# Attention on one NeuronCore: where TensorE makes the values of the four batches of a tile

## The reference

```
x = normalise(x * s1)                       # over the 512 features
q = heads(x @ q_weight.T * q_dc)
k = heads(x @ k_weight.T * k_dc)
v_flat = x @ v_weight.T * v_dc * s2;  v = heads(v_flat)
attn = softmax(q @ k.T * scale)             # 128 x 128 for each batch and head
out  = (attn @ v) @ w_weight.T * w_dc
skip = v_flat @ u_weight.T * u_dc
return out + skip
```

## Time and profile before

| | |
|---|---|
| Time, three runs | 4002.31, 4001.20, 3997.74 us; median 4001.2 |
| Profiled execution: span, first to last instruction | 3993.2 us (its own device time isn't listed; the median of the runs is 8.0 above the span) |
| TensorE busy over the span | 3737.8 us, 94% |
| VectorE busy | 3026.1 us, 76% |
| ScalarE busy | 1334.5 us, 33% |
| GpSimd busy | 1896.0 us, 47% |
| Mean granted clock of TensorE | 0.959 |

### The profile page before, as it was taken

How to read it: one execution, slowest core, us unless ns; L and a number is a source line. 1 busy time by engine, 2 the same in 40 slices (tenths; PEclk the granted TensorE clock), 3 DMA queues, 4 the chain that set the end, 5 groups by cost and what they waited for, 6 DMA issues and landing times. The chain is left out here.

```text
span 3993.2 us, 63716 instructions
## 1 busy us (share of the span) xinstructions
PE 3737.8 (94%) x22068; PEld 2291.3 (57%) x22068; DVE 3026.1 (76%) x3176; ACT 1334.5 (33%) x2014; POOL 1896.0 (47%) x1446
## 2 busy tenths in 40 slices
PE   8999769999998789999999999988999859999999
PEld 6777523433333567777777777766777613433334
DVE  4776679999997677777777777744666679999997
ACT  3555411111111444344434444323555501111111
POOL 2655635555554124444444444342555735555554
PEclk9999859999999799999999999999999959999999
DMA  3666755565653323222322222223666765565563
GB/s 121 236 240 246 286 200 169 183 194 173 187 187 120 112 90 128 78 80 79 107 88 91 80 80 80 67 78 121 227 238 245 275 223 169 175 193 179 183 194 112
DMA packets 272125, 630.18 MB, mean 158 GB/s; under 512 B 33216, under 2 KB 35904, under 8 KB 271840
## 3 DMA queue, kind: packets, MB, share of 16 engines
q1 hardware_dynamic: 264816, 615.49, 46.3%
q10 hardware_dynamic: 7104, 11.93, 0.8%
HBM read 390.87 MB, written 241.70 MB: 158 GB/s over the span
## 5 line engine op out<-in xcount | busy, mean ns | idle before, releaser
L1164 DVE CUSTOM_DVE_ANT_0 l0r_g<-l0r_g,l0r_pv,l0r_cf 128x1024 f32<-128x1024 f32 x512 | 674.1, 1339 | 70.4 <-PE l0r_pv L964 46.7
L1164 DVE CUSTOM_DVE_ANT_0 l3r_g<-l3r_g,l3r_pv,l3r_cf 128x1024 f32<-128x1024 f32 x512 | 673.9, 1339 | 68.3 <-PE l3r_pv L964 43.6
L102 PE MATMUL l1h_ps_p<-l1h_xh,l1c_wh 128*128 128x512 f32 x768 | 322.6, 420 | 5.7 <-issue 3.5
L104 PE MATMUL l1h_ps_p<-l1h_xl,l1c_wh 128*128 128x512 f32 x768 | 308.2, 401 | 0.0
L103 PE MATMUL l1h_ps_p<-l1h_xh,l1c_wl 128*128 128x512 f32 x768 | 305.4, 398 | 0.0
L2152 POOL TENSOR_TENSOR l1h_st<-l1h_veps 128x1 f32<-128x1 f32 x64 | 35.4, 554 | 565.5 <-DVE l1h_veps L2010 565.5
L964 PE MATMUL l3r_pv<-l3r_x,l3r_wv 32*128 32x512 f32 x1024 | 260.4, 507 | 25.0 <-POOL l3r_wv L884 17.4
L964 PEld LDWEIGHTS l0r_pv<-l0r_x,l0r_wv 32*128 32x128 f32 x1024 | 97.2, 187 | 324.7 <-issue 205.0
L964 PEld LDWEIGHTS l3r_pv<-l3r_x,l3r_wv 32*128 32x128 f32 x1024 | 96.5, 186 | 324.7 <-issue 191.8
L964 PE MATMUL l0r_pv<-l0r_x,l0r_wv 32*128 32x512 f32 x1024 | 261.7, 510 | 22.5 <-POOL l0r_wv L884 16.4
L976 PE MATMUL l0r_py<-l0r_g,l0r_cd 128*32 128x512 f32 x2048 | 281.7, 624 | 0.0
(11 more groups left out here) (386 smaller groups left out, 9046.9 us busy)
## 6 DMA issues: line engine op xcount, KB each, us to landing
l0r_x<-xhl_s SPq DMA_DIRECT2D x128, 512.0 KB, 11.4
l3r_x<-xhl_s SPq DMA_DIRECT2D x128, 512.0 KB, 11.6
xhl_s<-l0a_xo SPq DMA_DIRECT2D x116, 512.0 KB, 4.6
xhl_s<-l3a_xo SPq DMA_DIRECT2D x116, 512.0 KB, 4.6
gate_s<-l0a_gate SPq DMA_DIRECT2D x64, 256.0 KB, 2.5
l0r_dx<-dx_s SPq DMA_DIRECT2D x32, 512.0 KB, 13.2
l0r_gate<-gate_s SPq DMA_DIRECT2D x32, 512.0 KB, 13.9
l0r_crow<-feed_s SPq DMA_DIRECT2D x64, 256.0 KB
```

The costliest lines, as they stand in the source:

```text
L102: pe.matmul(out, wh, xh, start=first, stop=False)
L104: return pe.matmul(out, wh, xl, start=False, stop=last)
L1164: dve._custom_dve(bass.dve_ops.TENSOR_ADD_SAT, out=g[:, t, j, :], in0=g[:, (t - 1) % TS, j, :], in1=pv[j % 2][:, :], s0=cf[:, q, t, 0, j:j ...
```

## The change

In TensorE's `period(p)` two calls move. values(g, 0) goes from ahead of turn(g, 1) to directly ahead of values(g, 1), and values(g, 2) from ahead of turn(g, 3) to directly ahead of values(g, 3). The new order is: scores; turn 0; mix_u; turn 1; mix_w; values 0; values 1; turn 2; project Q; turn 3; project K; values 2; values 3; turn_v; project V. Waits go with their calls and stay as they are. No other engine is changed.

```diff
                 if sooner(p, "K"):
                     project(p, Q, "Q", q_mm)
-                values(g, 0)
                 turn(g, 1)
                 if burst:
                     turn_x(p, "X3")
@@
                     project(p, K, "K", k_mm)
                 elif sooner(p, "Q"):
                     project(p, Q, "Q", q_mm)
+                values(g, 0)
                 values(g, 1)
                 turn(g, 2)
                 if not sooner(p, "Q"):
                     project(p, Q, "Q", q_mm)
                 if extra(p):
                     next_sum_rows(p)
-                values(g, 2)
                 turn(g, 3)
                 if not sooner(p, "K"):
                     project(p, K, "K", k_mm)
                 if extra(p):
                     next_add_rows(p)
+                values(g, 2)
                 values(g, 3)
                 turn_v(p)
                 project(p, V, "V", v_mm)
```

## The result

| | before | after |
|---|---|---|
| Median | 4001.76 us (4 runs) | 3978.39 us (4 runs) |
| Ratio | | 0.9944, 95% interval 0.9929 to 0.9958 |
| Profiled execution, span | 3993.2 us | 3981.8 us |
| First to last scores of the attention stage (rows below) | 1284.3 us | 1262.2 us |
| TensorE busy | 3737.8 us | 3707.3 us |

The forecast was 3975.7 in a range of 3969 to 3989. The change makes the kernel 0.56% faster, 22 us by the ratio (17 to 28).

A forecast was written before the change was run, and what follows sets the result against it. TensorE was taken to bound the attention stage, except burst heads, which go at VectorE's pace. 106 pairs at 0.27 us (-28.6), -0.7 for the last tiles and +3.8 paid gave -25.5: 3975.7 us, range 3969 to 3989.

The forecast's parts named there:

- What bounds the stage: Attention stage: TensorE busy 1338 of 1400 us, all of an ordinary period; time taken from its stream leaves the total.
- The group taken out, 0.51: Between mix_u and mix_w in an ordinary period: removing a values group saves 1.41 - 0.90 = 0.51 us.
- The group put in, 0.24: A values group directly beside another group costs 0.13 + 0.11 = 0.24 us, bounds 0.20 to 0.36.
- First pairs of the bursts: Values 0 leave time VectorE's pace hides in burst heads: 14 cost 0.24 us each, the weight swap's nothing.
- Periods 1, 2, 4 and 5: Second pairs: 0.24 us cost each in periods 1 and 2, nothing in 3 to 5; other pairs gain 0.27.
- Second pairs of the last tiles: Last two tiles: turn 3 goes first, values 2 run during ScalarE's last copy, saving 0.36 us each.
- The sum: Whole kernel: -28.6 - 0.7 + 3.8 = -25.5 us; by the bounds -10.8 to -30.4.
- the covers of batch 1's copy: Values 1 and turn 2 wait for ScalarE's copy of batch 1, with 1.3 us of cover.
- The time around the span: Whole execution: 8.0 us taken to lie between the profiled span of 3993.2 us and the median of 4001.2.
- Rival 1: Second values group costs 0.36 us, its weight loads not overlapping the first's matmuls; -10.8 us, 3990.4; chance 0.06.
- Rival 2: VectorE or ScalarE sets ordinary periods' pace; only the last tiles' 0.7 us stay, 4000.5; chance 0.05.
- Rival 3: Clock falls in bursts behind longer TensorE gaps: +22 us and 4023, or a loss of 24; chance 0.04.

The follow-up runs named there:

- the kernel with the groups apart: Against the kernel before: values 0 behind mix_w, then turn 2, values 1; turn 3, values 2, project K, values 3; ratio 1.0026 (1.0014 to 1.0039).
- the second timing: The changed kernel itself timed once more, nothing altered, against the kernel before; ratio 0.993 (0.9912 to 0.9948).
- one run of four groups: Against the changed kernel: ScalarE's copies kept in e, all four values groups together behind project K; ratio to the kernel before 0.992 (0.99 to 0.9941).
- the two kernels with the run next to the scores: All four values groups behind project V, copies in e: ratio 0.9907 to the kernel before; the second also copies batch 2 sooner, ratio 0.9863.
- the last kernel: Against the kernel with all values behind project V: ScalarE copies batch 2 ahead of high parts of v and o; 3951.0 us, 0.9863 to before.

## Why the prediction was right, point by point

- **What bounds the stage.** Right: TensorE is busy all of an ordinary period before and after, and what its stream lost came out of the time. "No wait is removed" was wrong by the traces, which have 64 wait instructions less (1164 for 1228); it made no difference, since the kernel with the groups apart has 96 less and is slower.
- **The group taken out, 0.51.** Right: 0.50 in the timeline.
- **The group put in, 0.24 within 0.20 to 0.36.** Measured 0.22: with values 0 alone moved the burst gets longer by it, and keeping values 0 in the burst's head takes it back. The second group's first wave has nothing of an entry in it, so my 0.13 for it was 0.02 too much. A pair brings 0.29, where I said 0.27. With the groups apart the gain is gone (19.58), so it is the change of form that is paid. The 0.29 is what the prediction worked out by the rule of the Trainium skill in TensorEngine Tiling (Array Packing), Key Properties, that TensorE is drained when the tiling mode changes and not when only the tile does; the trace agrees.
- **First pairs of the bursts.** Right in kind and size: 21.55 to 21.47 for the burst shown, +0.22 for the first pair and -0.28 for the second.
- **Periods 1, 2, 4 and 5.** The second pairs of 1 and 2 cost 0.2 each, as said. The first pairs of all four were counted at 0.27 and brought nothing: with values 0 alone moved, these periods stay within 0.1 us of before. That is 1.1 us too much in the sum.
- **Second pairs of the last tiles.** Right: period 63 of after has the order that I drew, turn 3 at 2623.93 behind the copy and values 2 right behind the turn, at 2624.49. From the last scores to the last values it is 22.96 us where it was 24.12.
- **The sum.** -25.5 forecast, -22 measured (17 to 28 less), -28 in the second timing (21 to 35 less). By the pair's measured 0.29 and 0.22 for a group that is paid it would be -28, so the number came out close in part because errors cancel. By the starts of the scores the profiled execution loses, against that sum, some 5 us at the stall of periods 47 and 48, the 1.1 of the four first pairs above, and 0.9 in period 38, which has a new wait: turn 3 stands 0.71 us for ScalarE's copy of batch 2.

```profile
2129.10 0.63 PE L1637 MATMUL l1h_ps_t<-l1h_ident,l1h_e 128*128 128x128 f32 x4 [0.71 <-ACT l1h_pt L1764]
```

VectorE does the swap's low part of W just before (3.26 us from 2115.54) and is late with that tile's softmax. I had named the covers of batch 1's copy, and not that of batch 2's for turn 3; it is what one run of four groups ran into in ordinary periods. On the other side two bursts got shorter by more than a pair's worth. Period 7 went from 25.47 us in both traces of before to 23.96 and 23.98, and period 31, with the first weights of the swap, from 27.73 to 26.54 and 25.71. In both the clock fell less: over period 7 it is 0.93 before and 1.00 after, over period 31 0.88 and 0.94 or 1.00. So it isn't one execution's luck. But I had left out that the change could raise the clock, and no run shows what in it does.
- **The time around the span.** The 8.0 us was wrong in kind: the profiled execution of after spans 3981.8 us and took 3983.86, so 2 us lie around it. By the same 2 us (an estimate) before's profiled execution took about 3995, less than any of its timed runs. This did not touch the forecast, since span and 8.0 add up to the median.
- **Rival 1** (the second group's weight loads don't overlap with the first group's matmuls, 0.36): out. Two groups need 0.22 more than one and not 0.36, and all 16 loads of a run lie within 0.38 us, beside matmuls that span 0.64:

```profile
1924.14 0.38 PEld L1647 LDWEIGHTS l1h_ps_o<-l1h_pt,l1h_v 128*32 128x32 f32 x16 [0.36 <-issue]
```

The sentence in the Trainium skill, TensorE: Matmul & The Clock Gate, The mechanism, that loads overlap with matmuls in flight only in other row groups, does not hold for these 32-column tiles: the measurement decides. The same section also lets a load go ahead into the background weight buffer, which the prediction left out; these loads would fit that, though no run shows which buffer they go to.
- **Rival 2** (another engine's pace): out in ordinary periods. **Rival 3** (the clock): out, it stays at 1.00 over the bursts with the wait of 0.60 us, period 7 among them; only over the swap's (period 31) one trace has 0.94, where before has 0.88.

## What to carry to other kernels

Where a stream on TensorE is dense, count how often it changes its form (32-column, 32-row, full array), not only its matmuls: each run of 32-column matmuls cost 0.29 us here above its own two waves of 0.11, and small groups that can wait belong side by side, next to another narrow form if there is one. Before moving work, look whether it stands in time that another engine's pace leaves over: there it is free, and moved away it is paid. And list the cover of every later wait, not only of the moved one: sooner work eats the margin of the next (here batch 2's copy), and a reorder on the other engine can give it back. Last, look where the loop steps back: a change of order alone took some 5 us there.

## What I had not expected of the hardware

A reorder of TensorE's stream, with the same matmuls and fewer wait instructions, lengthened the wait at one step back of its loop from 0.4 and 0.6 us to 3.3 and stopped the engine in the middle of the scores; the two kernels with the run next to the scores have over 8 us of such waits in all. And the direct change from 32-column to 32-row matmuls costs 0.17 us less than the two changes by way of the full array (18.45 against 18.62 us). In the last kernel the run next to the scores starts 0.32 us behind a full matmul and the scores follow 1.01 us behind its start, four groups at 0.22 and 0.13 more:

```profile
1924.00 0.39 PE L104 MATMUL l1h_ps_p<-l1h_xl,l1c_wh 128*128 128x512 f32 x1
1924.32 1.08 PE L1646 MATMUL l1h_ps_o<-l1h_e,l1h_v 128*32 128x128 f32 x32
1925.33 0.39 PE L1623 MATMUL l1h_ps_s<-l1h_kt,l1h_qt 32*128 32x128 f32 x4
```
